# A graph layer's edge pass on ScalarE: float16 pairs copied as int32 words, and constant biases in the selector passes

## The reference

```python
def step(carry, a):                      # layer 0, 128 rows of adj at a time
    mask = a != 0
    masked = jnp.where(mask[:, :, None], x[None, :, :], neg)
    m = jnp.max(masked, axis=1)
...
h = jnp.maximum(_layernorm(x, axis=-1), 0.0)
x = x + _L0_gnn_ref(h, adj)              # neighbour maximum
h = jnp.maximum(_layernorm(x, axis=-1), 0.0)
x = x + _L1_gnn_ref(h, adj, L1_gnn_W, L1_gnn_a)   # e = leaky_relu(h a1 + h a2), softmax over neighbours, @ h W, elu
```

## Time and profile before

| | value |
|---|---|
| median of three runs | 789.96 us |
| span of the profiled execution | 788.3 us |
| TensorE busy (matmul) | 702.4 us, 89% |
| VectorE busy | 722.4 us, 92% |
| ScalarE busy | 488.4 us, 62% |
| GpSimd busy | 285.7 us, 36% |
| edges pass, 128x1024 from uint16 | 128 times, 1023 ns each |
| `first` pass, 128x1024 with a per-partition bias | 128 times, 1113 ns each |
| `depth` pass, the same | 128 times, 1107 ns each |
| fold, 128x512 (VectorE) | 8 times, 681 ns each |
| name, 128x6 (VectorE) | 32 times, 162 ns each |

### The profile page before, as it was taken

One profiled execution on the slowest core, in us unless ns is written; L12 is line 12 of the kernel. 1 busy time (PEld: TensorE's weight loads), 2 busy tenths in 40 slices (PEclk: granted clock), 3 DMA queues, 4 the chain that ended last, 5 costly groups with the idle time before them and its releaser, 6 DMA issues.

```text
span 788.3 us, 14774 instructions
## 1 busy us (share of the span) xinstructions
PE 702.4 (89%) x5592; PEld 481.2 (61%) x5592; DVE 722.4 (92%) x1127; ACT 488.4 (62%) x618; POOL 285.7 (36%) x258
## 2 busy tenths in 40 slices
PE   1688999999999999999999999789899999999994
PEld 1344444444444444444444444369899999999994
DVE  8899889999999999999999999998999799998893
ACT  2978888888888888888888888455333221011000
POOL 0612033443443443443344344353340085143040
PEclk9999999999999999999999999999999999999998
DMA  9799777997777777777778764624442435434500
GB/s 304 240 369 367 271 234 222 275 324 222 256 234 227 259 224 237 261 213 247 251 212 258 240 213 111 229 68 135 158 148 107 161 134 174 171 129 155 173 17 17
DMA packets 62857, 162.56 MB, mean 206 GB/s; under 512 B 6400, under 2 KB 11136, under 8 KB 58688
## 3 DMA queue, kind: packets, MB, share of 16 engines
q1 hardware_dynamic: 53776, 138.75, 51.1%
q0 software_dynamic: 9008, 22.82, 12.2%
HBM read 117.51 MB, written 44.04 MB: 205 GB/s over the span
## 4 chain that ended last, share of the span: by engine, by line
PE 46%; DVE 23%; ACT 19%; issue 8%; DMA 2%; POOL 1%; ACTq 0%; DVEq 0%; SPq 0%
PE pick_ps L678 21%; PE pick_ps L578 9%; DVE acc L830 9%; ACT edge_t L373 8%; PE order_ps L559 6%; ACT depth L382 6%; DVE rest L1009 6%; ACT first L381 4%; PE late_ps L591 3%; PE late_ps L550 3%; DVE rest L819 2%; DMA subset_max<-keys 2%; PE late_ps L587 1%; POOL h_lo L316 1%; DMA best<-x 1%
## 5 line engine op out<-in xcount | busy, mean ns | idle before, releaser
L830 DVE TENSOR_TENSOR acc<-pick_ps,acc 128x1024 f32<-128x1024 f32 x248 | 302.8, 1221 | 27.4 <-PE pick_ps L578 20.5
L345 POOL DMA_INDIRECT found<-subset_max,entry x192 | 208.3, 1085 | 300.3 <-DVE entry L842 198.8
L1009 DVE SCALAR_TENSOR_TENSOR rest<-depth,curves_sb,stage 128x512 f32<-128x512 f32 x256 | 199.7, 821 | 14.7 <-PE pick_ps L678 2.3
L678 PE MATMUL pick_ps<-keys,rest 128*128 128x129 f32 x1792 | 207.0, 276 | 5.2 <-DVE rest L1009 5.2
L678 PEld LDWEIGHTS pick_ps<-keys,rest 128*128 128x128 f32 x1792 | 203.3, 192 | 9.7 <-DVE rest L1009 8.0
L381 ACT ACTIVATE first<-order_ps,neg 128x1024 f16<-128x1024 f32 x128 | 142.5, 1113 | 61.2 <-PE order_ps L559 59.6
L382 ACT ACTIVATE depth<-order_ps,mid 128x1024 f16<-128x1024 f32 x128 | 141.6, 1107 | 0.0
L373 ACT ACTIVATE edge_t<-late_ps 128x1024 f16<-128x1024 uint16 x128 | 131.0, 1023 | 2.9 <-PE late_ps L550 2.9
L559 PE MATMUL order_ps<-edge_t,order_w 128*128 128x512 f16 x256 | 78.7, 390 | 38.5 <-ACT edge_t L373 31.3
L578 PE MATMUL pick_ps<-first,h_hi 128*128 128x512 f16 x256 | 97.5, 381 | 8.5 <-DVE acc L830 8.5
L578 PE MATMUL pick_ps<-second,h_hi 128*128 128x512 f16 x256 | 97.5, 381 | 2.5 <-DVE acc L830 2.4
(11 more groups left out here) (140 smaller groups left out, 578.2 us busy)
## 6 DMA issues: line engine op xcount, KB each, us to landing
stage<-adj SPq DMA_DIRECT2D x64, 1024.0 KB
edge_units<-edge_t SPq DMA_DIRECT2D x64, 512.0 KB
stage<-edge_units SPq DMA_DIRECT2D x32, 1024.0 KB, 4.9
subset_max<-keys POOLq DMA_DIRECT2D x12, 512.0 KB, 9.2
found<-subset_max,entry POOLq DMA_INDIRECT x192
best<-x SPq DMA_DIRECT2D x4, 512.0 KB, 6.3
subset_max<-x POOLq DMA_DIRECT2D x4, 512.0 KB, 9.2
out<-keys POOLq DMA_DIRECT2D x7, 256.0 KB, 3.2
```

Of the source, the lines that this page charges most:

```text
L345: nc.gpsimd.indirect_dma_start(found[:, n % NG, s, :], None, subset_max, bass.IndirectOffsetOnAxis(entry[:, n, s:s + 1], 0)).then_inc(gath ...
L678: last = nc.tensor.matmul(out_ps(q, b), weight[:, n % WEIGHTS, b * P:(b + 1) * P], wh[:, c, :], start=c == 0 and starts(q, b), stop=c == C ...
L830: V.tensor_tensor(acc[:, q % 2, :], pick_ps[k][:, :], acc[:, q % 2, :], ALU.max).then_inc(raised, 1)
L1009: V.scalar_tensor_tensor(out=weight[:, n % WEIGHTS, :], in0=limit[:, q % 4, :], scalar=slope[:, c:c + 1], in1=units[:, m % EDGES, k * TI:( ...
```

## The change

The edges pass now sees the bank of turned edges as 512 int32 words, each two float16 values. It copies them to `edge_t`, also seen as int32, with a scale of 15360, which is the bit pattern of float16 1.0 (0x3C00). A word of 0x00010001 becomes 0x3C003C00. The same bytes are read and written as before, by half as many elements, with `Copy` in place of `Sign`. The passes `first` and `depth` take their bias as a constant in the instruction, where they read it from a 128x1 column of on-chip memory. The two columns and the two memsets that filled them at the start are gone. No instruction is moved, no wait is added or removed, and no transfer is changed.

```diff
-        neg = sb("neg", [P, 1], F32)
-        mid = sb("mid", [P, 1], F32)
...
-        flip_ps, key_ps = late_ps[:, 0:TI].bitcast(F16), late_ps[:, TI:W]
+        flip_ps, flip_i, key_ps = late_ps[:, 0:TI].bitcast(F16), late_ps[:, 0:TI].bitcast(I32), late_ps[:, TI:W]
...
-                    nc.scalar.activation(edge_t[:, g % (KEPT * KEEP), :], flip_ps[:, :].bitcast(U16), ACT.Sign).then_inc(edge_ready, 1)
+                    nc.scalar.activation(edge_t[:, g % (KEPT * KEEP), :].bitcast(I32), flip_i[:, :], ACT.Copy, scale=ONE_BITS).then_inc(edge_ready, 1)
...
-                    nc.scalar.activation(first[:, g % 4, :], order_ps[:, :], ACT.Relu, scale=-1.0, bias=neg[:, :]).then_inc(first_ready, 1)
-                    nc.scalar.activation(depth[:, g % 4, :], order_ps[:, :], ACT.Abs, bias=mid[:, :]).then_inc(depth_ready, 1)
+                    nc.scalar.activation(first[:, g % 4, :], order_ps[:, :], ACT.Relu, scale=-1.0, bias=1.0 - MARK).then_inc(first_ready, 1)
+                    nc.scalar.activation(depth[:, g % 4, :], order_ps[:, :], ACT.Abs, bias=MARK - MID).then_inc(depth_ready, 1)
...
-                V.memset(neg[:, :], 1.0 - MARK)
-                V.memset(mid[:, :], MARK - MID)
```

More of the change, by code:

```diff
@@ L4 @@
 from contextlib import ExitStack
-F32, F16, I32, U16 = mybir.dt.float32, mybir.dt.float16, mybir.dt.int32, mybir.dt.uint16
+F32, F16, I32 = mybir.dt.float32, mybir.dt.float16, mybir.dt.int32
 ALU, ACT, AX = mybir.AluOpType, mybir.ActivationFunctionType, mybir.AxisListType
@@ L23 @@
 HSCALE = 4096.0
+ONE_BITS = 15360.0
 QUAD = 4
```

## The result

The changed kernel takes 755.53 us (median of four runs, 754.77 to 755.73) against 790.1 us (median of four too): a ratio of 0.9555, 95% interval 0.9544 to 0.9567, 34.6 us less. One term that I had put at nothing, the start, brought 1.5 us.

What follows compares the result with a forecast made beforehand. A ring of waits through ScalarE and rank bounds pairs 18 to 124; VectorE's floor comes next. Gains of 29.9 and 1.9 us, less 1.5, bring the span from 788.3 to about 758.0; plus 1.66, 759.7 us, range 756 to 772.

Steps and rivals of the forecast that it cites:

- The ring: Pairs 18 to 124: ScalarE's first, depth, edges, then hand-over and rank; 3.73 us a pair, 3.12 after the change.
- The price of an int32 pass: ScalarE's edges pass with 512 elements: 0.61 us for 1.02, 0.41 less, all of it in the ring.
- Biases: ScalarE's first and depth without a per-partition operand: each saves about 0.10 us.
- VectorE's floor: Summed from start-to-start distances of VectorE's operations: 13.67 us for four pairs, 3.42 a pair, the next bound after the ring.
- The rival that VectorE was full already: VectorE's places last whole durations, so almost nothing is gained: 788 to 790 us, chance 0.04.
- TensorE, and the two in each other's way: TensorE's floor 3.27 us a pair, under VectorE's by 4%; rival: late picks keep about 3.56, 771 us, chance 0.09.
- Pairs 11 to 17: Ahead of pair 18 TensorE is the next bound: take(18,0) at 98.37 instead of 100.23 us, 1.9 less.
- Transfers: DMA share rises from 0.75 to 0.82, at 255 GB/s; costed at nothing, else flip would wait for a load.
- What I would see: Signs in the changed profile, among them first following first after about 3.4 us, idling for rank above 0.9 us.
- Before 75.75 us I count nothing: Early part: VectorE is full, and a lead ends in the chain step that waits 1.7 us for a DMA.
- For hand-overs that do not fit so closely I give back 1.5 us: Allowance taken off the 31.8 us gain, about 0.014 us a pair, an estimate.
- After pair 125 I count nothing: Behind pair 125 no gain; from 515.44 us on, the attention layer, 272.86 us, shifts as a whole.

Runs made afterwards that it cites:

- The biases alone: Only the constant biases of first and depth, edges as before, against the kernel before: 770.33 us, ratio 0.9746.
- the memsets: One idle 128x256 VectorE memset more in each of pairs 18 to 124: 777.65 us on the changed kernel, 789.25 us on the kernel before.
- The runs: The change from pair 6 on only: 756.84 us; in pairs 0 to 5 only: 788.77 us; each against the kernel before.
- the late load: Changed kernel with one more SyncE wait, so the seventh adjacency load goes out only with the sixth edges pass: 758.86 us.
- the kernel with the name on ScalarE: Changed kernel with the name cast of tiles 0 to 25 moved from VectorE to ScalarE: 758.21 us.
- the buffer alone: Changed kernel plus an unused buffer of 4 KB a partition, which moves the addresses of the buffers behind it: 755.84 us.

## Where the prediction held, and the step of it that failed

- **The ring.** Right. The biases alone shorten it to 3.55 us (I had 3.53 for a ring without the edges' part), with its waits unchanged.
- **The price of an int32 pass.** Right: 604 ns for 0.61 us, with half the elements of the old pass. (The key pass is not the fastest of this size in the trace: those of line L406, in the attention layer, take 0.59 us.) Biases: about 0.09 us each for 0.10. The memsets did save nothing, but not for the reason given: VectorE does not idle behind them, and their 0.06 us are gone one operation later (2.16 us after, 2.15 before).
- **VectorE's floor.** Right: 13.65 us for four pairs against 13.67, and the memsets show that it is the floor. The rival that VectorE was full already fell; successors start 1.13 us into a take of 1.22 here too. The Trainium skill, page "VectorE: DVE Perf Modes", section "The DRAIN you can't avoid", has both the rule that the next operation waits until the pipe is empty and the exception for operations that are not held; these starts agree with the exception.
- **TensorE, and the two in each other's way.** No pick was late from pair 18 on, with 4% between the floors.
- **Pairs 11 to 17.** 1.7 us came for 1.9.
- **Transfers.** DMA share 0.79 at 254 GB/s for the 0.82 at 255 I had, and no flip of the 107 pairs waited for a load.
- **What I would see.** The idling in front of `first` was to be above 0.9 us; it is 0.76 in the mean (81.2 us over 107 pairs), since in every other pair the key pass fills part of it (0.66 or 0.21 for 1.05).

The step that failed is "Before 75.75 us I count nothing", with its reason that a lead ends in the chain step that waits for a DMA. It was 1.5 us. I had treated the end of that transfer as a fixed time, so that only VectorE's own lead (0.45 us at take(4,1)) was to be had and lost in the wait. But the transfer itself landed earlier: the wait fell from 1.72 to 0.64 us although VectorE came to it sooner. The runs show that the gain belongs to the first six pairs, and that it goes when the seventh adjacency load goes out 1.9 us later. That the load counts because the queues were idle before 36 us and full after fits the DMA shares; the late load missed my number for it (51.9 us for 50 to 50.6), so how the 1.5 us divide among the transfers stays open.

The other terms are sizes. "For hand-overs that do not fit so closely I give back 1.5 us": nothing had to be given back. The 107 pairs took 368.4 us for 369.3, 0.9 less. "After pair 125 I count nothing" left out 0.6. With 0.2 too much in pairs 11 to 17 these make the 4.3 us by which the span came out under the forecast (753.7 for 758.0). The range's lower end, 756, left 3.7 us below the forecast, less than these terms together. Without the 1.5 us at the start the time would have been about 757.1 us, inside the range.

## What to carry to other kernels

Before pricing a faster pass, find the ring it stands in and the next floor under it, made from start-to-start distances: the gain is the distance between the two, however much more the pass saves. The end of a transfer need not be a fixed wall: here it moved by 1.5 us with the change, and ahead of it the queues had idled. Before a lead is counted as lost in such a wait, look whether the same change makes transfers go out earlier too. And terms put at their cautious value one by one make a range that is too high as a whole.

## What the runs showed of the hardware that I had not expected

- Two takes in a row, the second waiting for the first, start 1.33 us apart, and a name or a short halve between them (0.16 or 0.28 us long) leaves the distance at 1.32 to 1.33. Here such small work between two dependent operations is free.
- A 128x256 memset of 0.27 us costs 0.21 us a pair where VectorE is full.
- A VectorE operation can last longer beside work of GpSimd. In the twelve kernels that keep GpSimd's order, chain step 1 lies wholly beside GpSimd's subtractions and lasts 1.22 to 2.20 us; chain steps 2 to 4, where none of these runs, last 1.21 to 1.22. Takes beside the same subtractions never last over 1.23.
- A seconds pass of 0.69 us took 0.83 to 0.84 us in all 18 cases in which it spanned the gap between two gathers of GpSimd in the kernel with the name on ScalarE. No seconds or rests pass of any kernel's stretch took over 0.73 us without such a gap. A gap is not enough by itself: four passes in other kernels spanned one and took 0.68 to 0.74.
- The attention layer was 1.4 to 1.9 us shorter in three profiled runs: of both kernels with memsets in the first stage (271.0 for 272.9 and 271.3 for 272.7) and of the one with the name on ScalarE (271.1). No operation of that layer was changed in any of them, and the buffer alone did not repeat it. It stays open.
